# Sorting tokens to experts and running the experts: two blocks made one, with other row buffers

## The reference

```python
logits = jnp.einsum('blh,he->ble', x, Wr) + br
top_expert = jnp.argmax(logits, axis=-1)
mask = jax.nn.one_hot(top_expert, NUM_EXPERTS, dtype=x.dtype)     # 4 experts
for e in range(NUM_EXPERTS):
    h1 = jax.nn.relu(jnp.einsum('blh,hf->blf', x, We1[e]) + be1[e])   # 128 -> 512
    oe = jnp.einsum('blf,fh->blh', h1, We2[e]) + be2[e]               # 512 -> 128
    out = out + mask[..., e:e + 1] * oe
```

## Time and profile before

| what | us |
|---|---|
| median of 3 runs | 3239.93 (3236.76 to 3244.71) |
| profiled execution | 3235.5 |
| its span in the profile | 3233.8 |

### The profile page before, as it was taken

The page is one execution under the profiler, slowest core; times in us unless marked ns, Lnnn a source line. Parts: engine busy times, 40 slices in busy tenths (PEclk is TensorE's granted clock), DMA queues, the critical chain, the costliest instruction groups (busy, mean ns, idle before and its releaser), DMA issues. The chain is left out here.

```text
span 3233.8 us, 61215 instructions
## 1 busy us (share of the span) xinstructions
PE 2509.6 (78%) x18663; PEld 1043.7 (32%) x18790; DVE 2597.0 (80%) x4291; ACT 2238.7 (69%) x2389; POOL 1999.9 (62%) x1358
## 2 busy tenths in 40 slices
PE   1464899998365897488888888888888888883799
PEld 1452333333354454222222222222222222222455
DVE  4446888886555666699999999999999999997665
ACT  2242477777143453289999999999999999992454
POOL 3430122222433454099999999999999999993454
PEclk9986799999586899689999999999999999996799
DMA  3113110110011000200000000000000000000000
GB/s 107 40 53 98 31 30 27 29 29 12 31 43 44 1 1 0 89 12 16 11 12 14 11 13 13 11 15 11 11 15 11 13 14 11 14 1 1 4 11 13
DMA packets 76210, 74.71 MB, mean 23 GB/s; under 512 B 15984, under 2 KB 56440, under 8 KB 75968
## 3 DMA queue, kind: packets, MB, share of 16 engines
q1 hardware_dynamic: 71552, 63.94, 6.8%
q0 software_dynamic: 4544, 9.35, 0.9%
HBM read 48.04 MB, written 24.42 MB: 22 GB/s over the span
## 5 line engine op out<-in xcount | busy, mean ns | idle before, releaser
L1746 POOL TENSOR_TENSOR a_sg<-a_sg,a_shifted 128x1664 f32<-128x1664 f32 x256 | 955.6, 3733 | 21.4
L1943 DVE TENSOR_REDUCE a_mx<-a_pm 128x1 f32<-128x1024 f32 x512 | 619.8, 1210 | 21.6 <-PE a_pm L1785 21.6
L1952 DVE TENSOR_SCALAR a_sg<-a_pa 128x1024 int32<-128x1024 int32 x512 | 619.9, 1211 | 3.6 <-PE a_pa L1785 3.3
L1865 ACT ACTIVATE a_pt<-a_pb 128x1024 f32<-128x1024 f32 x512 | 524.0, 1023 | 107.9 <-PE a_pb L1785 107.9
L1802 PE MATMUL a_po<-a_pt,a_Vh 128*32 128x512 f32 x2048 | 539.1, 605 | 2.2 <-ACT a_sg L1884 2.2
L1802 PE MATMUL a_po<-a_sg,a_Vh 128*32 128x512 f32 x2048 | 539.1, 605 | 0.0
L1743 POOL TENSOR_SCALAR a_shifted<-a_sg,a_parh 128x1664 f32<-128x1664 f32 x256 | 469.5, 1834 | 102.6 <-DVE a_sg L1952 63.9
L1880 ACT ACTIVATE a_sg<-a_sg,a_parh 128x2048 f32<-128x2048 f32 x256 | 511.9, 2000 | 0.0
L1884 ACT ACTIVATE a_sg<-a_sg 128x2048 f32<-128x2048 f32 x256 | 489.8, 1913 | 0.0
L1785 PE MATMUL a_pm<-all_K,all_Q 96*128 96x512 bf16 x1024 | 316.2, 391 | 150.7 <-DVE a_mx L1943 124.6
L1564 ACT ACTIVATE a_pt<-a_ring 128x1024 f32<-128x1024 f32 (+2 forms) x384 | 313.7, 846 | 167.6 <-PE a_ring L1491 164.3
(11 more groups left out here) (278 smaller groups left out, 4763.7 us busy)
## 6 DMA issues: line engine op xcount, KB each, us to landing
all_Q<-q_parts SPq DMA_DIRECT2D x256, 48.0 KB
all_K<-k_parts SPq DMA_DIRECT2D x256, 48.0 KB
k_parts<-p_parts SPq DMA_DIRECT2D x16, 384.0 KB, 2.5
all_Q<-a_rows SPq DMA_DIRECT2D x384, 2.0 KB
e_recs<-routed_rows SPq DMA_DIRECT2D x70, 64.5 KB, 1.9
n_xn<-expert_rows SPq DMA_DIRECT2D x8, 512.0 KB, 6.6
q_parts<-p_parts SPq DMA_DIRECT2D x16, 192.0 KB, 2.3
q_parts<-p_parts SPq DMA_DIRECT2D x8, 384.0 KB, 2.5
```

The lines of the kernel that those rows point to most:

```text
L1746: nc.gpsimd.tensor_tensor(buf[:, :, 0:CUT], buf[:, :, 0:CUT], shifted[:], ALU.mult)\
L1865: nc.scalar.activation(pt[(j - LT) % 4][:, i, :], pb[:], ACT.Exp, scale=SC)\
L1943: nc.vector.tensor_reduce(mx[:, (j // PER) % 2, t:t + 1], pm[:], AX.X, ALU.max)\
L1952: nc.vector.tensor_scalar(sg[(j - LS) % 4][:, i, :].bitcast(I32), pa[:].bitcast(I32), SIGN_OFF, None, ALU.bitwise_and).then_inc(abs_done, 1)
```

## The change

`dispatch` and `experts` become one function, `route_experts`, with one block and one clearing of semaphores; the tile loop's code stands behind the sorting code on every engine. In PSUM, psx and psh are now views of sorting's `pt`, and psy of `psr`. The number of row buffers R goes from 6 to 12. The normalised rows are written by ScalarE (Identity with a scale and a bias per row; VectorE makes the bias, -mean x scale, as `away`). VectorE's order in step s is now statistics(s), scales(s-1), choose(s-3), locate(s-4). The padding rows behind each expert's tokens are sent by SyncE, by plain DMAs at a row number in a register. SyncE, no longer a block's end, waits for the table, its own DMAs and all token scatters before the first row load. `ln_transposed` loads `expert_rows` in 8 pieces of 4 tiles (NCH = 8) and adds piece by piece.

```diff
-        came = [m.sem(f"came{g}") for g in range(G)]
+        came = [m.sem(f"came{g}") for g in range(NCH)]
...
-                        t = slice(g * GT, (g + 1) * GT)
-                        dve.wait_ge(came[g], 16)
-                        nc.vector.tensor_tensor(X[:, t, :], X[:, t, :], xn[:, t, :], ALU.add).then_inc(summed, 1)
-                        dve.wait_ge(summed, g + 1)
+                        for c in range(g * GT // 4, (g + 1) * GT // 4):
+                            t = slice(4 * c, 4 * c + 4)
+                            dve.wait_ge(came[c], 16)
+                            nc.vector.tensor_tensor(X[:, t, :], X[:, t, :], xn[:, t, :], ALU.add).then_inc(summed, 1)
+                        dve.wait_ge(summed, (g + 1) * GT // 4)
...
+    R, S = 12, len(returned)
...
+        psx, psh = pt[:, 0:2, :], pt[:, 2:4, :]
+        psy = psr[:].rearrange("p b t n -> p b (t n)")
...
-                    for k in range(g * GT, (g + 1) * GT):
-                        nc.vector.tensor_scalar(rec[:, k, 0:D], X[:, k, :], mv[:, k, 0:1], rstd[:, k:k + 1],
-                                                ALU.subtract, ALU.mult).then_inc(xn_ready, 1)
+                    nc.vector.scalar_tensor_tensor(away[:, tiles], mv[:, tiles, 0], -1.0, rstd[:, tiles],
+                                                   ALU.mult, ALU.mult).then_inc(away_ready, 1)
...
-                for s in range(G + 3):
+                for s in range(G + 4):
                     if s < G:
                         statistics(s)
                     if 0 <= s - 1 < G:
-                        normalise(s - 1)
-                    if 0 <= s - 2 < G:
-                        choose(s - 2)
+                        scales(s - 1)
                     if 0 <= s - 3 < G:
-                        locate(s - 3)
+                        choose(s - 3)
+                    if 0 <= s - 4 < G:
+                        locate(s - 4)
...
-                pool.wait_ge(pads_placed, 1)
-                for e in range(E0):
-                    nc.gpsimd.indirect_dma_start(
-                        rows_d, bass.IndirectOffsetOnAxis(ap=pad_place[:, e:e + 1], axis=0), pad[:, e, :], None)\
-                        .then_inc(sent, 16)
-                pool.wait_ge(sent, 16 * (NT + E0) * (n + 1))
...
             def _(sp):
...
-                sp.wait_ge(sent_spare, 16)
+                sp.wait_ge(pads_placed, 1)
+                for e in range(E0):
+                    tail = sp.value_load(pad_row[0:1, e:e + 1], min_val=0, max_val=E0 * REGION - P)
+                    sp.dma_start(rows_d[bass.ds(tail, P), :], pad[:, e, :]).then_inc(sent_spare, 16)
+                sp.wait_ge(tab_ready, 2)
+                sp.wait_ge(sent_spare, 16 * (1 + E0))
+                sp.wait_ge(sent, 16 * NT * (n + 1))
+
+                for j in range(SLOTS0):
+                    row = sp.value_load(tab[0:1, 0, j:j + 1], min_val=0, max_val=ROWS - P)
+                    if j >= R:
+                        sp.wait_ge(rows_turned, j - R + 1)
+                        sp.wait_ge(*back(j - R))
+                    sp.dma_start(recs[:, j % R, :], rows_d[bass.ds(row, P), :]).then_inc(loaded[j % R], 16)
...
             def _(act):
...
+                def normalise(g):
+                    act.wait_ge(away_ready, g + 1)
+                    for k in range(g * GT, (g + 1) * GT):
+                        nc.scalar.activation(rec[:, k, 0:D], X[:, k, :], ACT.Identity, bias=away[:, k:k + 1],
+                                             scale=rstd[:, k:k + 1]).then_inc(xn_ready, 1)
+
+                for s in range(G + 2):
+                    if s < G:
+                        tiles = slice(s * GT, (s + 1) * GT)
...
+                    if 0 <= s - 1 < G:
+                        normalise(s - 1)
+                    if 0 <= s - 2 < G:
+                        evacuate(s - 2)
...
-        m.clear_sems()
-
-
-def experts(nc, tag, ident, w, f0w, rows_d, y_d, tab, returned, n):
-
-
-    pick = w[2]
-    R, S = 6, len(returned)
```

More of the change, by code:

```diff
@@ L380, in dispatch, with inside, back @@
             m.sem(x) for x in ("routed", "choice", "chosen", "counted", "hit", "placed"))
-        ids_set, pad_ready, pads_placed, sent_spare, ones_set, table = (
-            m.sem(x) for x in ("ids", "pad", "padsplaced", "sentspare", "ones", "table"))
+        ids_set, pad_ready, pads_placed, sent_spare, ones_set, table, tab_ready, away_ready = (
+            m.sem(x) for x in ("ids", "pad", "padsplaced", "sentspare", "ones", "table", "tabready", "away"))
+        recs = m.sb("recs", [P, R, REC])
+        slot = m.sb("slot", [P, S, FW], F16)
+        xh = m.sb("xh", [P, 3, P], F16)
+        xl = m.sb("xl", [P, 3, P], F16)
+        hid = m.sb("hid", [P, 2, F0])
+        hidh = m.sb("hidh", [P, 3, F0], F16)
+        hidl = m.sb("hidl", [P, 3, F0], F16)
+        ysb = m.sb("ysb", [P, S, D])
+        psx, psh = pt[:, 0:2, :], pt[:, 2:4, :]
+        psy = psr[:].rearrange("p b t n -> p b (t n)")
+        loaded = [m.sem(f"loaded{r}") for r in range(R)]
+        rows_turned, xh_done, xl_done, slot_in, h_done, hid_done, high_done, low_done, y_done, y_out = (
+            m.sem(x) for x in ("rturned", "xh", "xl", "slotin", "h", "hid", "high", "low", "y", "yout"))
+        stages = range(SLOTS0 + 3)
+        def inside(j):
+            return 0 <= j < SLOTS0
+        def back(j):
+            r = j % S
+            return returned[r], 16 * (n * len(range(r, SLOTS0, S)) + j // S + 1)
         with nc.Block() as block:
@@ new lines, in high_x, with relu @@
+                def high_x(j):
+                    act.wait_ge(rows_turned, j + 1)
+                    if j >= 3:
+                        act.wait_ge(h_done, j - 2)
+                    nc.scalar.activation(xh[:, j % 3, :], psx[:, j % 2, 0:P], ACT.Copy).then_inc(xh_done, 1)
+                def relu(j):
+                    act.wait_ge(h_done, j + 1)
+                    if j >= 3:
+                        act.wait_ge(y_done, j - 2)
+                    if j >= 2:
+                        act.wait_ge(low_done, j - 1)
+                    nc.scalar.activation(hidh[:, j % 3, :], psh[:, j % 2, :], ACT.Relu, scale=1.0 / WSCALE)\
+                        .then_inc(high_done, 1)
+                    nc.scalar.activation(hid[:, j % 2, :], psh[:, j % 2, :], ACT.Relu, scale=1.0 / WSCALE)\
+                        .then_inc(hid_done, 1)
@@ new lines, in result @@
+                def result(j):
+                    act.wait_ge(y_done, j + 1)
+                    if j >= S:
+                        act.wait_ge(*back(j - S))
+                    nc.scalar.activation(ysb[:, j % S, :], psy[:, j % 2, 0:D], ACT.Copy, scale=0.5 / WSCALE)\
+                        .then_inc(y_out, 1)
+                for s in stages:
+                    if inside(s):
+                        high_x(s)
+                    if inside(s - 1):
+                        relu(s - 1)
+                    if inside(s - 3):
+                        result(s - 3)
@@ L666, in output @@
                         .then_inc(y_done, 1)
-                for s in steps:
+                for s in stages:
                     if inside(s):
-                        turn(s)
+                        turn_row(s)
                     if inside(s - 1):
```

190 lines of the change are left out of this document (59 added, 131 removed).

## The result

Over four runs each, the changed kernel took 3131.69 us (3129.78 to 3134.51) and the kernel before 3238.35 (3236.51 to 3244.71). The ratio is 0.9673, with a 95% interval of 0.9661 to 0.9685: 106.7 us faster, where 3134 us was forecast. The profiled execution took 3132.6 us, its span is 3130.8, and the mean granted clock is 0.931 (0.929 before).

A forecast was written before the change was run, and what follows sets the result against it. Waits were taken to bound sorting and tile loop. 15.5 + 39.1 + 6.3 + 9.2 + 58.0 + 13.9 = 142.0 us per network, saving 54.3 and 50.0, plus 1.2 from additions: 105.5 us less, 3134 us forecast, range 3118 to 3164.

The forecast's parts named there:

- The terms 15.5 and 39.1: Sorting: 15.5 us from start to first scatter, then 39.1 us for 31 intervals of 1.26 us, bound by GpSimd.
- The rival of a wait for logits: Sorting stays bound by waiting for logits: 49.1 us between scatters, not 39.1; 20 us more, 3154 us; chance 0.07.
- 0.96 + 2.5 + 0.9: Last token scatter to first turn: scatter, landing and register, which with 1.9 from load to turn gave 6.3 us.
- the last rival: Tile loop slower through four result buffers: round trip 4.5 us, deciding beyond 8; at 17 us, 3265 us; chance 0.02.
- One block: Sorting and tile loop merged: last token scatter to first turn takes 6.3 us for 14.2.
- the bounds of 1.84 and 2.12: Tile loop, us per tile: 1.84 from the opening tiles' copies, 2.12 if every copy fully holds up a scatter.
- the rival that scatters bound the loop: Tile loop: copies and scatters never overlap, 2.12 us per tile, 7 us more, 3141 us; at 2.3, 3151; chance 0.15.
- no wait of SyncE on results: Tile loop, a sign of success: SyncE would no longer wait for result scatters, which had stopped it for 60.5 us.
- the rival on the slow side: Tile loop: the ring of four result buffers decides, with landings of 15 us giving 3265 us; chance 0.02.
- the rival of the lower clock: Tile loop: TensorE's matmuls start 0.11 us apart, 3.2 us per tile, 70 us more, 3204 us; chance 0.03.
- The clearing at the end stays: End of the merged block: semaphore clearing remains, with the tail left at 13.9 us.
- the tail 13.9 us: From turn 34 to the load following the network: taken as unchanged at 13.9 us.

The follow-up runs named there:

- the middle drain: Changed kernel, in which GpSimd also waits for the 32 token scatters and drains once before the first result scatter; 3125.23 us, ratio 0.9665.

## Why the prediction was right

**Sorting.** The terms 15.5 and 39.1 came out as 15.7 and 39.5, and by their reason: from 56.86 to 96.31 the 31 steps take 1.26 us each (the first 1.48, two 1.31), so GpSimd bounds sorting. The prices under it were less good. Four rows took ScalarE 1.65 us (0.41 each, inside the bounds of 0.2 to 0.5) and not 0.9, VectorE's period is about 4.05 us and not 3.7 to 3.9, and its wait before the logits reaches 1.17 in these rows and 1.78 at 73.88, not "under 1 us":

```profile
54.40 0.17 DVE L445 TENSOR_TENSOR e_score<-e_psr,all_br 128x16 f32<-128x16 f32 x1
54.52 1.65 ACT L589 ACTIVATE e_rec<-all_X,e_away,e_rstd 128x128 f32<-128x128 f32 x4 [0.43 <-DVE e_away L436]
...
62.53 0.17 DVE L445 TENSOR_TENSOR e_score<-e_psr,all_br 128x16 f32<-128x16 f32 x1
...
67.07 0.17 DVE L445 TENSOR_TENSOR e_score<-e_psr,all_br 128x16 f32<-128x16 f32 x1 [0.92 <-PE e_psr L653]
...
70.60 0.17 DVE L445 TENSOR_TENSOR e_score<-e_psr,all_br 128x16 f32<-128x16 f32 x1 [1.17 <-PE e_psr L653]
```

The four periods from 54.40 to 70.60 are 16.2 us. None of it shows, since a group of scatters takes 5.04. The rival of a wait for logits did not come.

**Padding rows.** SyncE sends them at 80.26 within 3.68 us (predicted 4.8), 16 us ahead of the last token scatter. They were hidden, and the run with GpSimd sending them confirms the 5.0 us saved (5.2 to the first turn).

**First turn.** 5.5 for 6.3: from the last scatter's start to SyncE's load are 3.54 us, where 0.96 + 2.5 + 0.9 were taken. The prediction counted the scatter twice, since the time to landing runs from its start. SyncE's wait for the scatters (L569) ends at 98.6, 2.3 us after 96.31, which is also the median landing of token scatters, and its first register load (L572) begins at 98.7:

```profile
L569 SPq EVENT_SEMAPHORE  x1: 28/28/28, 98.6 to 98.6; - x1
...
L572 SPq TENSOR_LOAD <-all_tab x3: 265/267/277, 98.7 to 101.4; - x3
```

From there to the load at 99.85 are 1.2 us, so the register costs what was taken for it and 0.96 too much stands in the sum; the same double count is in the 4.5 us of the last rival. Of the 8.7 us by which this piece shrank, under "One block" in the prediction, the block's own part is 3.0 by the run with two blocks; 5.1 are the four padding scatters, and the rest goes to the clearing and a drain that is 0.3 shorter.

**Tile loop.** 1.91 us per tile, between the bounds of 1.84 and 2.12, for 2.0 taken. The upper bound, the rival that scatters bound the loop, asked that a scatter be held up for the whole of a copy. By the rows above, a scatter with a whole copy in it takes 0.57 longer, not 0.86, and the one at 133.32 took 1.00 although a copy began 0.23 us before its end. The rule of the Trainium skill, "SBUF — State Buffer", Who interferes with whom, is that these two shut each other out for the whole instruction, whichever comes first. One half of it agrees with the trace: the scatter at 131.49 ends at 133.02, 0.13 us after the copy in it, and so do the 14 others of this loop with a copy in them (0.11 to 0.13), as if held until the copy is done. But only 0.54 + 0.13 us of it lie outside the copy, so 0.29 of its 0.96 went on inside, and the prediction's sum of the two lengths is too long by that. The other half does not agree: the copy begins 0.54 us into the scatter and takes its usual 0.86. The forecast "no wait of SyncE on results" is wrong in its words, since there are 17.1 us in 13 waits, but the loads it delays are early enough. Result scatters land 4.1 us after their start now (median, 4.5 at most) for 2.5 before. With ScalarE's copy and the handover, the round trip of four result buffers stays under the 8 us from which that ring decides, so the rival on the slow side didn't come either. Nor did the rival of the lower clock: it is 1.00 in the loop. In the kernel before, the starts of matmuls went to 0.107 us apart six times between turns 5 and 34, for some 3 us each, and the granted clock of such a stretch is 0.50 (139.5 to 142.6, after 3 us in which TensorE was busy for 0.08). Now they do so only in the opening, from 103.17 to 106.59, as before from 125.71 to 129.02; there the profile's clock reads 1.00 all the same.

**The step that failed** is "The clearing at the end stays", with its term "the tail 13.9 us". It took 16.6 and 16.8 us, for 13.9 and 14.1 in the kernel before. The clearing did stay, but the end of a block holds GpSimd's drain, which grows with the number of indirect DMAs since the last drain: one block collects 67 where two had 36 and 35. That is 2.6 us per network that the one block gives back. The sum came out at 141.8 for 142.0 only because the first turn (-0.8) and the loop (-2.6) were overpriced by about as much as the tail (+2.7) and sorting (+0.6) were underpriced. That the total agrees within 0.2 us is luck: wrong terms with opposite signs stand behind it.

**The additions** gave 1.5 and 0.7 us for 0.6 each, as small as forecast; 1.0 and 0.6 of these go back with four pieces.

**Where the 106.7 us are.** Undone one at a time, buffers cost 66.1, the logits' place 33.8, padding rows 11.6, rows on ScalarE 3.8, pieces 3.3, one block -2.0: 116.6 together. The 10 us too many are ScalarE's normalising in the old order, which the kernel before did not have: (61.73 - 60.86) + (53.3 - 49.1) = 5.1 us per network. Counted against the kernel before, sorting to the last token scatter is shorter by 13.6 and 13.7 us, 27 together, of which the order alone brings some 24 (VectorE's normalising in the new order costs 1.5 per network). So of the 106.7 us the buffers bring some 66, sorting 27, the padding rows 11. The one block is worth nothing that the runs can tell as it stands, and about 5 us with the middle drain.

## What to carry to other kernels

Count what is in flight: a ring of R buffers whose slot frees k stages later has R - k tiles in flight, and the round trip divided by that is the price per tile, until the busiest engine's own period takes over (here at eight buffers). When an engine waits for the result of work that it started in the same step, move the reading one step later first. Here lifting work to another engine cost 5 us per network without that, and brought 1.5 with it. When blocks are merged, look for what their ends did per item (here a drain per indirect DMA), since it moves to the last end, and put it where other engines' work covers it.

## What the runs showed of the hardware

- GpSimd's drain takes 0.083 us per indirect DMA that it has issued since the last drain: 2.67 us for 32, 2.91 for 35, 3.01 for 36, 5.53 for 67, 5.86 for 71, although all of them have landed by then; 0.03 us with none.
- A scatter of GpSimd in which a copy of VectorE begins and ends takes 1.53 us for 0.96 (13 of the 15 in the first tile loop, the others 1.60 and 1.71) and ends 0.11 to 0.13 us after the copy. The copy takes its 0.86 us (median).
- 30 matmuls per tile, 29 of them with an operand at a register's address, take 3.84 us per tile with the loading of that register, with fixed addresses 1.91, at the same granted clock of 1.00. The wider steps between the matmuls are 1.1 us of it and the gap around the register's loading some 0.7. Whether the matmuls, the weight loads or the address arithmetic make the steps wider wasn't tried.
- Result scatters land 2.5 us after their start in the kernel before and 4.1 in the changed one (medians). The density of the loop is not the reason: at the same pace of 1.9 us per tile the medians are 2.5 with 8 buffers, 2.8 with 12 in the kernel before, and 2.9 with two blocks. Why is open; nothing in the trace waited longer for it.
